# State-space stage with 16 heads: its scores as 64-row products of two heads, its mixing as 32-column products of four heads

## Chip, core and metric

The kernel runs on one core of one Trainium2 chip. The time is that of one execution on the device in microseconds (us). Engines are named as in the profile: PE is the array for matrix products (PEld its weight loads), DVE the vector engine, ACT the engine for activation functions, POOL the general one, SP the queue that issues transfers.

## The reference, cut to what matters

A network of four layers runs over 16 sequences of 256 rows of 128 channels. The change touches one block of it, a state-space block with 16 heads, a state of 64 and an inner width of 256, so 16 channels a head. For head h and time steps t and s of one sequence:

    decay[h, s, t]  = exp(cum[h, t] - cum[h, s])   for s <= t, else 0     (cum: running sum of log decays)
    score[h, s, t]  = sum over 64 states of b[h, state, s] * c[h, state, t]
    y[h, d, t]      = sum over s of x[h, s, d] * decay[h, s, t] * score[h, s, t]        d = 0 .. 15
    out             = rms_norm(y * sigmoid(gate)) @ w_out

b, c, x, gate and the step sizes are projections of the normalised input; x also goes through a short causal convolution and silu. Nothing of this changes.

## The kernel before

The program is a row of stages; the edited one is made by `ssm_block(..., heads=16, mamba=False)`, whose tiles carry the prefix `ssm_`. A second stage, with 4 heads (`mamba=True`, prefix `mamba_`), comes from the same function. The stage works through eight pairs of sequences (PAIRS = 8). A pair has 512 rows: two sequences j = 0, 1 of 256, each two tiles of 128.

**Front part of a pair.** PE takes a list of work items in turn through two PSUM banks (`run_item`, lines 1048 to 1107): x (L1062), dt (L1064), sixteen bc items (L1067; eight for c, then eight for b), two gate items (L1069), two turns of x (L1079), and between them, late, turn_y and out (L1090, L1105) of the pair before. ACT and DVE empty the banks. A b item holds the 64 states of two heads below each other and goes to `b_rows` in one operation. A c item holds two heads in the same way, but L1263 writes it in two operations of 64 rows: the lower head to `c_rows[0:64, 0]`, the upper one to `c_rows[64:128, 1]`. The other halves of `c_rows` stay zero (memset at L1326). DVE meanwhile runs the convolution and the chain of running sums (L1388 to L1420), which ends in `parts`.

**Units.** A unit is one head of one sequence; 32 a pair (u = 16 j + h), 256 in all.

- The fade: six bf16 products (L1128, L1130, L1132, once for 256 and once for 128 columns) put cum[t] - cum[s] for the three blocks on and above the diagonal, 384 columns, into one of two banks `dbank[u % 2]`. ACT takes the exponential into `decay[u % 2]` (L1281).
- The scores: L1150 (256 columns) and L1151 (128 columns) into `gbank[u % 2]`. All 128 rows of `b_rows` are stationary, with two heads in them; the zeros of `c_rows` cancel the other head.
- The mixer: DVE multiplies decay and score, 128 x 384 (L1465), into `mixer[u % 2]`, then drains and signals `scores_taken`.
- The mixing: L1164 and L1165 add x times mixer for this head into `ybank`. Stationary is a 128-column tile of `x_wide` with the head's 16 channels in place and zeros in the other 112 columns. So the eight heads of a half (EACH = 8, CH = 2) accumulate into the same 128 rows of PSUM.

PE runs one unit ahead: `unit(u + 1)`, then `mix(u)` (L1185 to L1193). Float32 products show as two passes each in the profile (x2 in a row of the timeline), bf16 ones as one.

**Other work between the units.** After unit 15, DVE gates the first sequence (`take_gated`, L1353); ACT squares it after the decay of unit 17, and PE sums the squares (turn_y) ahead of the mixing of unit 19. In pairs 1 to 7, DVE does the tail of the pair before between mixers (L1472 to L1479): after u = 1 the scaling and the first norm's moments, after u = 4 the norm, the addition to x and the next moments, after u = 7 the next norm (`tail_at`, L927). PE turns that result after u = 10 and ACT stores it.

Four waits bound how far the engines run apart: ACT's decay of unit u waits for mixer u - 2, PE's fade of u for decay u - 2, PE's scores of u for mixer u - 2 (`scores_taken`), DVE's mixer of u for mixing u - 2 (`y_up`).

Of the kernel before, what the change touches and what calls it, by code (L numbers as in the profile page):

```python
# [15 lines left out]
ALU = mybir.AluOpType  # L16
ACT = mybir.ActivationFunctionType
# [883 lines left out]
def ssm_block(core, name, tail, heads, mamba):  # L901
# [26 lines left out]
    with ExitStack() as ctx:  # L928
# [13 lines left out]
        else:  # L942

            x_wide = sb("x_wide", [P, PT, CH, EACH * (P + HD)])

            b_rows, c_rows = sb("b_rows", [P, bc_items // 2, PN]), sb("c_rows", [P, 2, bc_items // 2, PN])
# [7 lines left out]
        decay, mixer = sb("decay", [P, 2, SPAN]), sb("mixer", [P, 2, SPAN])  # L954
# [87 lines left out]
        def _(pe):  # L1042
# [71 lines left out]
            def pair(i, has_late):  # L1114
# [3 lines left out]
                def unit(u):  # L1118

                    j, h = divmod(u, heads)  # L1120
                    n = i * units + u
# [3 lines left out]
                    if not (isinstance(i, int) and u < 2):  # L1125
                        pe.wait_ge(decay_done, n - 1)
# [7 lines left out]
                    if mamba and h:  # L1134
                        return
                    if mamba:
                        b, c = bc[0:STATE, 0, :], bc[0:STATE, 1, :]
                        turn_no = i * 2 + j
                        skip = isinstance(i, int) and j < 1
                        need = turn_no  # L1140
                        gb = gbank[0]
                    else:
                        b, c = b_rows[:, h // 2, :], c_rows[:, h % 2, h // 2, :]
                        skip = isinstance(i, int) and u < 2
                        need = n - 1
                        gb = gbank[u % 2]

                    if not skip:
                        pe.wait_ge(scores_taken, need)
                    pe.matmul(gb[:, 0:SEQ], b[:, s[0]:s[0] + P], c[:, s[0]:s[0] + SEQ], start=True, stop=True)  # L1150
                    pe.matmul(gb[:, SEQ:SPAN], b[:, s[1]:s[1] + P], c[:, s[1]:s[1] + P], start=True,  # L1151
                              stop=True).then_inc(scores_up, 1)

                def mix(u):
# [6 lines left out]
                    if not mamba:  # L1161
                        c, k = divmod(h, EACH)
                        x = [x_wide[:, 2 * j + t, c, k * P:(k + 1) * P] for t in range(2)]
                        pe.matmul(ybank[:, c * SEQ:(c + 1) * SEQ], x[0], m[:, 0:SEQ], start=(k == 0), stop=False)  # L1164
# [21 lines left out]
                for u in range(units):  # L1186
                    if u + 1 < units:
                        unit(u + 1)
# [2274 lines left out]
```

## Time and profile before

| | |
|---|---|
| median of 3 runs | 5105.25 us (5102.89 to 5107.88) |
| profiled execution, its own time | 5086.59 us |
| its span | 5084.6 us |
| busy: PE, PEld, DVE, ACT, POOL | 77%, 53%, 51%, 44%, 21% of the span |
| granted TensorE clock, mean | 0.863 of full speed |

The sum of the prediction is made against the profiled execution and carried over to the median. The stage lies from about 2676 to 3535 us. A busy PE is a modelled figure: the end of a matmul's row lies some tenths of a us after its columns are through, so starts of rows are compared, not ends. An engine's idle time stands in brackets, with what ended it.

### The profile page before, as it was taken

To read this page: it belongs to the slowest core of one execution; us is meant where nothing else is said; L and a number is where in the kernel's file an instruction comes from. 1 tells how busy PE (TensorE), PEld (TensorE's weight loads), DVE (VectorE), ACT (ScalarE), POOL (GpSimd) and SP (SyncE) were. 2 spreads that over 40 slices of the span, in tenths; PEclk is the share of its full clock that TensorE was granted. 3 is DMA by queue.
4 is the path that set the end of the run, shared out by engine and by line. 5 is a ranking of instruction groups with operands and counts; after the bars stand their busy time and mean duration, and the time that the engine had idled before them with its cause. 6 is when DMAs were issued, how large, how long until landed. Compare 5 with 4: busy or idle time off the path is not lost. (4 is left out here: it accounts for less than half of the span.)

```text
span 5084.6 us, 65295 instructions
## 1 busy us (share of the span) xinstructions
PE 3893.2 (77%) x19738; PEld 2713.3 (53%) x19800; DVE 2569.9 (51%) x6625; ACT 2231.9 (44%) x4312; POOL 1045.3 (21%) x1066
## 2 busy tenths in 40 slices
PE   3659954999967688878877888987999877720398
PEld 1137722677734455546555667765677555520266
DVE  5858744222234766477864343342222255579544
ACT  3446533333442688778863433342333333300133
POOL 1012211000001666366640000000000000154200
PEclk9879977899976799989998999998999966655599
DMA  1420021000000000000000000000000000000000
GB/s 38 76 51 7 6 75 54 1 0 0 0 20 0 18 1 0 1 18 1 0 1 16 1 0 0 0 0 33 1 0 0 5 1 0 0 1 0 18 0 17
DMA packets 45622, 58.55 MB, mean 12 GB/s; under 512 B 14058, under 2 KB 37836, under 8 KB 44588
## 3 DMA queue, kind: packets, MB, share of 16 engines
q1 hardware_dynamic: 38956, 50.63, 3.6%
q10 hardware_dynamic: 6528, 6.29, 0.8%
q8 instruction: 61, 1.00, 0.1%
q14 instruction: 77, 0.63, 0.0%
HBM read 34.87 MB, written 10.51 MB: 9 GB/s over the span
## 5 line engine op out<-in xcount | busy, mean ns | idle before, releaser
L418 PEld LDWEIGHTS bank<-moe_w,moe_hidden 128*128 128x128 f32 x5376 | 626.6, 192 | 78.6 <-issue 76.4
L418 PE MATMUL bank<-moe_w,moe_hidden 128*128 128x128 f32 x5376 | 630.3, 275 | 0.0
L408 PE MATMUL bank<-normed_t,moe_w 128*128 (+1 forms) x1344 | 613.9, 599 | 11.0 <-ACT moe_hidden L470 7.6
L470 ACT ACTIVATE moe_hidden<-bank,moe_b 128x512 f32<-128x512 f32 x544 | 372.8, 687 | 504.0 <-PE bank L408 502.5
L546 DVE SCALAR_TENSOR_TENSOR branch<-bank,moe_weights,branch 128x128 f32<-128x128 f32 x768 | 216.2, 344 | 708.1 <-PE bank L418 704.1
L90 POOL TENSOR_TENSOR branch_norm_shifted<-branch_norm_moments,eps 128x4 f32<-128x4 f32 x64 | 12.8, 200 | 1914.0 <-DVE branch_norm_moments L83 1914.0
L408 PEld LDWEIGHTS bank<-normed_t,moe_w 128*128 128x128 f32 x1344 | 244.3, 192 | 254.6 <-issue 239.3
L1960 POOL TENSOR_TENSOR local_size<-local_size,local_half_powers 128x8 f32<-128x8 f32 x128 | 257.2, 2009 | 199.7 <-DVE local_size L2026 195.7
L1465 DVE TENSOR_TENSOR ssm_mixer<-ssm_decay,bank 128x384 f32<-128x384 f32 x256 | 141.8, 554 | 300.8 <-PE bank L1151 263.2
L1281 ACT ACTIVATE ssm_decay<-bank 128x384 f32<-128x384 f32 x256 | 124.9, 491 | 327.4 <-PE bank L1132 327.3
L1664 PE MATMUL bank<-local_wqkv,local_shifted 128*128 128x512 f32 x384 | 211.8, 644 | 58.7 <-ACTq L1837 23.9
L843 PE MATMUL bank<-ident,attn_scaled 128*128 128x128 f32 x32 | 8.9, 432 | 250.0 <-DVE attn_scaled L808 250.0
L1848 ACT ACTIVATE local_probs<-bank,local_peak 128x128 f32<-128x128 f32 x512 | 182.1, 379 | 8.5 <-issue 8.4
L1067 PE MATMUL bank<-ssm_in_rows,ssm_wbc 128*128 128x512 f32 x256 | 142.7, 676 | 45.1 <-ACTq L1264 45.1
L1164 PE MATMUL bank<-ssm_mixer,ssm_x_wide 128*128 128x256 f32 x512 | 158.8, 392 | 19.5 <-DVE ssm_mixer L1465 19.5
L1150 PE MATMUL bank<-ssm_c_rows,ssm_b_rows 128*128 128x256 f32 x512 | 173.2, 421 | 0.0
L1952 POOL TENSOR_TENSOR local_turned_part<-local_raw,local_tables 128x512 f32<-128x512 f32 x128 | 165.8, 1295 | 28.0 <-ACT local_raw L1827 26.8
L1689 PE MATMUL bank<-local_k_t,local_q_t 128*128 128x128 f32 x1024 | 139.8, 281 | 23.7 <-ACT local_probs L1848 20.8
L1689 PEld LDWEIGHTS bank<-local_k_t,local_q_t 128*128 128x128 f32 x1024 | 139.4, 198 | 28.0 <-issue 20.8
L1965 POOL TENSOR_TENSOR local_probs<-local_probs,local_total 128x512 f32<-128x512 f32 x128 | 133.2, 1041 | 81.6 <-DVE local_total L2050 81.6
L2045 DVE TENSOR_REDUCE local_peak<-bank 128x4 f32<-128x512 f32 x128 | 88.5, 691 | 114.6 <-PE bank L1689 107.3
L470 ACT ACTIVATE moe_hidden<-bank 128x512 f32<-128x512 f32 x128 | 76.5, 597 | 152.1 <-PE bank L408 152.1
(535 smaller groups left out, 8933.4 us busy)
## 6 DMA issues: line engine op xcount, KB each, us to landing
rwkv_kept<-rwkv_keep SPq DMA_DIRECT2D x8, 768.0 KB, 15.2
moe_w<-in_moe_w_dram SPq DMA_DIRECT2D x2, 2304.0 KB
rwkv_gate<-rwkv_kept SPq DMA_DIRECT2D x8, 512.0 KB, 3.6
moe_w<-in_moe_w_dram SPq DMA_DIRECT2D x2, 2048.0 KB
rwkv_values<-rwkv_sent_v ACTq DMA_DIRECT2D x16, 128.0 KB
normed_t<-rwkv_sent_b SPq DMA_DIRECT2D x16, 128.0 KB
x<-rwkv_sent_w ACTq DMA_DIRECT2D x16, 128.0 KB
rwkv_recv<-rwkv_sent_r SPq DMA_DIRECT2D x16, 128.0 KB
```

What stands on the lines that cost most here:

```text
L408: pe.matmul(hbank[n % 4][:], w1[:, e, f * P:(f + 1) * P], source_t[:, bass.ds(i * PN, PN)], start=True, stop=True).then_inc(hidden_up, 1)
L418: last = pe.matmul(obank[e % 2][:, t * P:(t + 1) * P], hid[:, e % 2, f, t * P:(t + 1) * P], w2[:, e, f, :], start=(f == 0), stop=(f == chu ...
L470: act.activation(hid[:, e % 2, f, :], hbank[n % 4][:], ACT.Gelu_apprx_tanh, bias=b1[:, n:n + 1] if bias else 0.0).then_inc(hidden_done, 1)
L546: last = dve.scalar_tensor_tensor(core.branch[:, t, :], obank[e % 2][:, t * P:(t + 1) * P], weights[:, i * PT + t, e - first_routed:e - fi ...
L1067: last = pe.matmul(bank[0:rows, :], wbc[:, n, :], source, start=True, stop=True)
L1150: pe.matmul(gb[:, 0:SEQ], b[:, s[0]:s[0] + P], c[:, s[0]:s[0] + SEQ], start=True, stop=True)
L1164: pe.matmul(ybank[:, c * SEQ:(c + 1) * SEQ], x[0], m[:, 0:SEQ], start=(k == 0), stop=False)
L1664: pe.matmul(bank[:], shifted[:, at, t * P:(t + 1) * P], wqkv[:, part * INNER:(part + 1) * INNER], start=True, stop=True).then_inc(a_up, 1)
L1689: last = pe.matmul(bank[:, w * P:(w + 1) * P], q_t[:, j, c, w, :], keys, start=False, stop=(w == WINDOWS - 1))
L1848: last = act.activation(probs[:, u % 2, w, :], sbank[u % 2][:, w * P:(w + 1) * P], ACT.Exp, bias=peak[:, u % 2, w:w + 1], accum_out=total[ ...
L1952: pool.tensor_tensor(turned_part[:, m % 2, :].rearrange("p (h s d) -> p h s d", s=2, d=HD // 2), rows, sines.broadcast_to([P, HEADS, 2, HD ...
L1960: pool.tensor_tensor(part, part, half_powers[:], ALU.pow).then_inc(scaled, 1)
```

## The change

- `c_rows` loses its zero halves: [128, 8, 512] in place of [128, 2, 8, 512]. A c item is stored by one ACT operation of 128 rows, as a b item is. The memset on DVE goes.
- Scores of two heads h and h + 1 are issued together (`two_units`): their fades first, then products on rows 0 to 63 (into bank 0) and on rows 64 to 127 (into bank 1), long parts first. PE now waits on `mixer_done` for the bank; DVE's drain and its separate signal go.
- `x_wide` holds 32 columns a head: its own 16 and 16 zeros. `mixer` has 16 slots in place of 2. The mixing of eight heads is issued at once (`mix_octet`): 16 products with 32 stationary columns, four of them to rows 0, 32, 64 and 96 of `ybank` in turn. The two heads of a group of 32 rows accumulate. DVE waits for an octet's mixing, two octets back, once per eight units; PE mixes octet o after the block of units 8 (o + 1) + 2 and + 3 has been issued, the last one at the end of the pair.
- x is copied to `x_wide` by two half-size copies per item in place of one. Gating the first sequence moves from after unit 15 to after unit 20; squaring from 17 to 21, turn_y from 19 to 22, its store from 20 to 24; ACT's store of the turned tail from u = 10 to u = 12.

```diff
-            x_wide = sb("x_wide", [P, PT, CH, EACH * (P + HD)])
-            b_rows, c_rows = sb("b_rows", [P, bc_items // 2, PN]), sb("c_rows", [P, 2, bc_items // 2, PN])
+            x_wide = sb("x_wide", [P, PT, CH, EACH, 2 * HD])
+            b_rows, c_rows = sb("b_rows", [P, bc_items // 2, PN]), sb("c_rows", [P, bc_items // 2, PN])
...
-        decay, mixer = sb("decay", [P, 2, SPAN]), sb("mixer", [P, 2, SPAN])
+        decay, mixer = sb("decay", [P, 2, SPAN]), sb("mixer", [P, 2 if mamba else 2 * EACH, SPAN])
...
+                def two_units(u):
+                    fade(u)
+                    fade(u + 1)
+                    j, h = divmod(u, heads)
+                    s = [j * SEQ, j * SEQ + P]
+                    for part, (to, rows, width) in enumerate(((0, s[0], SEQ), (SEQ, s[1], P))):
+                        for k in range(2):
+                            if part == 0 and not (isinstance(i, int) and u < 2):
+                                pe.wait_ge(mixer_done, i * units + u + k - 1)
+                            low = slice(k * STATE, (k + 1) * STATE)
+                            last = pe.matmul(gbank[k][:, to:to + width], b_rows[low, h // 2, rows:rows + P],
+                                             c_rows[low, h // 2, rows:rows + width], start=True, stop=True)
+                            if part:
+                                last.then_inc(scores_up, 1)
+
+                def mix_octet(o):
+                    j, c = divmod(o, CH)
+                    pe.wait_ge(mixer_done, i * units + (o + 1) * EACH)
+                    if c == 0 and not (isinstance(i, int) and j == 0):
+                        pe.wait_ge(y_taken, i * 2 + j)
+                    for b in range(2):
+                        for part, (to, at) in enumerate(((slice(0, SEQ), slice(0, SEQ)),
+                                                         (slice(P, SEQ), slice(SEQ, SPAN)))):
+                            for g in range(EACH // 2):
+                                h = 2 * g + b
+                                last = pe.matmul(ybank[g * 2 * HD:(g + 1) * 2 * HD, c * SEQ + to.start:c * SEQ + to.stop],
+                                                 x_wide[:, 2 * j + part, c, h, :], mixer[:, (o % 2) * EACH + h, at],
+                                                 start=(b == 0 and part == 0), stop=(b == 1 and part == 1))
+                    last.then_inc(y_up, 1)
...
+                two_units(0)
+                for u in range(0, units, 2):
+                    if u + 2 < units:
+                        two_units(u + 2)
+                    if u % EACH == 0 and u:
+                        mix_octet(u // EACH - 1)
+                    if u == heads + 6:
                         item("turn_y", 0)
-                    mix(u)
-                    if u == tail_at[3] and has_late and tail.turned:
+                    if u == tail_at[3] and has_late:
                         tail.pe(pe, i - 1)
+                mix_octet(units // EACH - 1)
...
-                        for half in range(2):
-                            low = slice(half * STATE, (half + 1) * STATE)
-                            act.activation(c_rows[low, half, b - bc_items // 2, :], bank[low, :], ACT.Identity)
-                        act.drain()
-                        act.sem_inc(sign, 1)
+                        act.activation(c_rows[:, b - bc_items // 2, :], bank[:], ACT.Identity).then_inc(sign, 1)
...
-            if not mamba:
-                dve.memset(c_rows[:], 0.0)
...
-                        out = x_wide[:, :, c].rearrange("p t (h k) -> p t h k", k=P + HD)[:, :, :, 0:HD]
-                        ins = dve.tensor_copy(out, bank.rearrange("p t (h d) -> p t h d", d=HD))
+                        own = x_wide[:, :, c].rearrange("p t (g b) k -> p t g (b k)", b=2)
+                        new = bank.rearrange("p t (g b d) -> p t g b d", b=2, d=HD)
+                        for b in range(2):
+                            at = b * 3 * HD
+                            ins = dve.tensor_copy(own[:, :, :, at:at + HD], new[:, :, :, b, :])
...
-                    if u >= 2:
+                    if mamba and u >= 2:
                         dve.wait_ge(y_up, n - 1)
-                    ins = dve.tensor_tensor(mixer[:, u % 2, :], decay[:, u % 2, :], scored, ALU.mult)
-                    ins.then_inc(mixer_done, 1)
-                    if not mamba:
-                        dve.drain()
-                        dve.sem_inc(scores_taken, 1)
-                    if u == heads - 1:
+                    if not mamba and u % EACH == 0 and u >= 2 * EACH:
+                        dve.wait_ge(y_up, i * 2 * CH + u // EACH - 1)
+                    slot = u % 2 if mamba else u % (2 * EACH)
+                    dve.tensor_tensor(mixer[:, slot, :], decay[:, u % 2, :], scored, ALU.mult).then_inc(mixer_done, 1)
+                    if u == (heads - 1 if mamba else heads + 4):
                         take_gated(i, 0)
```

## Rows read from the trace of the kernel before

**Rows 1.** The page, part 1: busy us, share of the span, instructions of each engine.

```profile
PE 3893.2 (77%) x19738; PEld 2713.3 (53%) x19800; DVE 2569.9 (51%) x6625; ACT 2231.9 (44%) x4312; POOL 1045.3 (21%) x1066
```

**Rows 2.** Windows: units of pairs 0 and 1, busy time, clock, DMA.

```profile
core 0: us, PE busy (x) PEld busy (x) DVE busy (x) ACT busy (x) POOL busy (x), PEclk, DMA share, GB/s
2724.60:2787.10 62.50, 62.05 (x456) 56.47 (x456) 18.84 (x34) 16.40 (x34) 0.00 (x0) 0.96 0.00 1
...
2825.60:2891.00 65.40, 62.34 (x460) 56.34 (x460) 25.07 (x63) 18.07 (x36) 2.42 (x4) 0.98 0.00 1
```

**Rows 3.** Timeline of one steady unit: start us, us, engine, line, operation.

```profile
2737.35 0.28 PE L1128 MATMUL bank<-ssm_parts,ssm_pick 96*128 96x256 bf16 x1
...
2737.75 0.22 PE L1132 MATMUL bank<-ssm_future,ssm_ident 128*128 128x128 bf16 x1
2737.81 0.65 PE L1150 MATMUL bank<-ssm_c_rows,ssm_b_rows 128*128 128x256 f32 x2
2738.29 0.38 PE L1151 MATMUL bank<-ssm_c_rows,ssm_b_rows 128*128 128x128 f32 x2
2738.51 0.60 PE L1164 MATMUL bank<-ssm_mixer,ssm_x_wide 128*128 128x256 f32 x2
2738.71 0.55 DVE L1465 TENSOR_TENSOR ssm_mixer<-ssm_decay,bank 128x384 f32<-128x384 f32 x1 [1.26 <-PE bank L1151]
2738.95 0.38 PE L1165 MATMUL bank<-ssm_mixer,ssm_x_wide 128*128 128x128 f32 x2
2739.17 0.28 PE L1128 MATMUL bank<-ssm_parts,ssm_pick 96*128 96x256 bf16 x1
2739.28 0.27 PE L1130 MATMUL bank<-ssm_unpick,ssm_parts 96*128 96x256 bf16 x1
```

**Rows 4.** Timeline of pair 1's first units, DVE first, then PE.

```profile
2829.63 0.55 DVE L1465 TENSOR_TENSOR ssm_mixer<-ssm_decay,bank 128x384 f32<-128x384 f32 x1 [0.49 <-PE bank L1151]
...
2832.94 0.55 DVE L1465 TENSOR_TENSOR ssm_mixer<-ssm_decay,bank 128x384 f32<-128x384 f32 x1 [0.26 <-issue]
...
2835.67 0.55 DVE L1465 TENSOR_TENSOR ssm_mixer<-ssm_decay,bank 128x384 f32<-128x384 f32 x1 [1.31 <-PE bank L1151]
...
2840.21 0.55 DVE L1465 TENSOR_TENSOR ssm_mixer<-ssm_decay,bank 128x384 f32<-128x384 f32 x1 [0.26 <-issue]
...
2843.69 1.11 DVE L99 TENSOR_SCALAR fresh<-x,x_norm_moments,x_norm_rstd 128x128 f32 x4 [0.21 <-issue]
...
2840.81 0.70 PE L1164 MATMUL bank<-ssm_mixer,ssm_x_wide 128*128 128x256 f32 x2 [1.56 <-DVE ssm_mixer L1465]
...
2848.82 0.27 PE L1128 MATMUL bank<-ssm_parts,ssm_pick 96*128 96x256 bf16 x1
```

**Rows 5.** Timeline of PE in the stage with 4 heads, a change of tile shape.

```profile
4229.56 0.22 PE L1132 MATMUL bank<-mamba_future,mamba_ident 128*128 128x128 bf16 x1
...
4230.24 0.38 PE L1151 MATMUL bank<-mamba_bc 64*128 64x128 f32 x2
...
4230.67 0.27 PE L1130 MATMUL bank<-mamba_unpick,mamba_parts 96*128 96x256 bf16 x1
```

**Rows 6.** Timeline of PE, one idle stretch; then windows, as rows 2, at half clock.

```profile
2796.26 2.08 PE L1067 MATMUL bank<-ssm_in_rows,ssm_wbc 128*128 128x512 f32 x2 [4.23 <-ACTq L1264]
...
2794.70:2804.90 10.20, 8.38 (x28) 6.61 (x29) 7.12 (x14) 4.37 (x9) 2.02 (x3) 0.50 0.00 1
4078.00:4112.00 34.00, 28.29 (x120) 21.70 (x120) 11.03 (x34) 5.81 (x11) 1.56 (x4) 0.50 0.00 1
```

**Rows 7.** Timeline of pair 1's front: a c item on ACT, bc items on PE.

```profile
2808.07 1.20 ACT L1263 ACTIVATE ssm_c_rows<-bank 64x512 f32<-64x512 f32 x2 [0.16 <-issue]
...
2812.06 6.85 PE L1067 MATMUL bank<-ssm_in_rows,ssm_wbc 128*128 128x512 f32 x14 [0.23 <-ACTq L1264]
```

**Rows 8.** Timeline: copies to x_wide, the stage's memset; DMA issues, us to landing.

```profile
2824.14 1.29 DVE L1447 COPY ssm_x_wide<-bank 128x512 f32<-128x512 f32 x2 [4.50 <-PE bank L1079]
...
2678.33 7.77 POOL L1018 MEMSET ssm_x_wide<- 128x9216 f32 x1
...
ssm_future<-in_future_dram SPq DMA_DIRECT2D x1, 32.0 KB, 4.0
```

More of the change, by code:

```diff
@@ L1116, in item, with fade @@
                     run_item(i, kind, n)
-                def unit(u):
+                def fade(u):
                     j, h = divmod(u, heads)
-                    n = i * units + u
                     s = [j * SEQ, j * SEQ + P]
@@ L1133, in unit @@
                     last.then_inc(decay_up, 1)
-                    if mamba and h:
+                def unit(u):
+                    fade(u)
+                    j = u // heads
+                    if u % heads:
                         return
[L1136 to L1151, printed above, removed]
-                              stop=True).then_inc(scores_up, 1)
+                    if not (isinstance(i, int) and u < heads):
+                        pe.wait_ge(scores_taken, i * 2 + j)
+                    b, c, s = bc[0:STATE, 0, :], bc[0:STATE, 1, :], [j * SEQ, j * SEQ + P]
@@ L1184, in pair @@
                     pe.wait_ge(down[side], before + 1)
-                unit(0)
-                for u in range(units):
-                    if u + 1 < units:
-                        unit(u + 1)
-                    if u == heads + (0 if mamba else 3):
+                if mamba:
+                    unit(0)
+                    for u in range(units):
+                        if u + 1 < units:
+                            unit(u + 1)
+                        if u == heads:
+                            item("turn_y", 0)
+                        mix(u)
+                        if u == tail_at[3] and has_late and tail.turned:
+                            tail.pe(pe, i - 1)
+                    return
+                two_units(0)
[5 more added lines that the diff above has]
+                    if u == heads + 6:
                         item("turn_y", 0)
-                    mix(u)
-                    if u == tail_at[3] and has_late and tail.turned:
+                    if u == tail_at[3] and has_late:
                         tail.pe(pe, i - 1)
+                mix_octet(units // EACH - 1)
             pair(0, False)
@@ L1281, in pair @@
                     act.activation(decay[:, u % 2, :], dbank[u % 2][:, 0:SPAN], ACT.Exp).then_inc(decay_done, 1)
-                    if u == heads + 1 and not mamba:
+                    if u == heads + 5 and not mamba:
                         square(i, 0)
-                    if u == heads + (1 if mamba else 4):
+                    if u == heads + (1 if mamba else 8):
                         turned_y(i, 0)
-                    if u == tail_at[3] and has_late and tail.turned:
+                    if u == tail_at[3] + (0 if mamba else 2) and has_late and tail.turned:
                         tail.act(act, i - 1)
@@ L1344, in take_gated @@
             def take_gated(i, j):
-                dve.wait_ge(y_up, i * units + (j + 1) * heads)
+                dve.wait_ge(y_up, i * units + (j + 1) * heads if mamba else i * 2 * CH + (j + 1) * CH)
                 if mamba:
```

14 lines of the change are left out of this document (5 added, 9 removed).

## The prediction

> **What bounds the kernel now.** I read, in this order: the page's busy times, the windows of single stretches, the timeline of one unit, the lines around the same operations in the other state-space stage, and the timelines of DVE and ACT. Over the whole span no engine but PE is near full [rows 1], but that is an average over eight stages; only one of them is edited. In it each of the eight pairs has a front part (projections, convolution) and 32 units. In the units of pair 0 PE is busy 62.05 of 62.50 us, DVE 18.84, ACT 16.40; in pair 1, 62.34 of 65.40, DVE 25.07, ACT 18.07 [rows 2]. So the array bounds the units. One steady unit lasts 1.82 us from L1128 to L1128: 0.46 for the six bf16 products of the fade (2737.35 to 2737.81), 0.70 for the scores (to 2738.51), 0.66 for the mixing (to 2739.17) [rows 3]. Every float32 product is two passes; from L1164 to L1165 is 0.44, so a pass of 256 columns costs 0.22, one of 128 costs 0.11. Nothing waits in this chain: time goes with streamed columns, whether rows of the array carry zeros (scores) or columns do (mixing). In pairs 1 to 7 the remaining 3 us come from DVE's tail work: the mixing at 2840.81 waited 1.56 us for the mixer [rows 4].
>
> **The fade** is untouched: 0.46 a unit.
>
> **Scores.** A block of two units now issues four products, tile 0, tile 1, then the short ones. Serially their passes are 4 x 0.22 + 4 x 0.11 = 1.32, what two units cost now (less the 0.05 that the first load sticks out). The trace has no two products in flight on different rows, so I bound it. Above: 1.32, no overlap. Below: if tiles ran with no regard to order, half, 0.66. Between: PE starts passes in program order [rows 3], and the second pass of a product needs the tile of its first; then only second pass and next product's first overlap. That gives starts 0, 0.22, 0.22, 0.43, 0.43, 0.54, 0.65, 0.76 and an end at 0.87; if each 128-column load (one pass of 128 columns long, estimate 0.11, since L1165's passes with their loads follow every 0.11) starts only with the previous pass, 1.08. I take 0.97.
>
> **Mixing.** An octet is 16 products of 32 stationary columns. Serially 8 x (0.44 + 0.22) = 5.28, as now. With neighbours overlapping as above, 8 x (0.22 + 0.11) = 2.64, plus up to 0.03 a product for the short loads: 3.1. I take 2.85. Four at a time without regard to order would be 1.32.
>
> The Trainium skill ("TensorE: Matmul & The Clock Gate", Part 3) reports matmuls on distinct row or column groups starting some 4 ns apart, with 2.38x for three column tiles and 3.07x for four row tiles; by its span model alone scores and mixing would take the lower ends. No run here shows this yet, and it does not speak of products made of two passes.
>
> **Change of tile shape.** The stage with 4 heads already has 64-row scores between full-height products. From L1132 to L1151 there is 4229.56 to 4230.24, 0.68; without a change of shape 2737.75 to 2738.29, 0.54. Going in costs 0.14. From L1151 to L1130 is 4230.24 to 4230.67, 0.43; from L1165 to L1130 2738.95 to 2739.28, 0.33. Going out costs 0.10 [rows 3, 5]. The Trainium skill ("TensorEngine Tiling (Array Packing)", Key Properties) says that changing the mode drains TensorE: a rule against this change, and the trace agrees, at 0.1 us a time. A block then costs 2 x 0.46 + 0.14 + 0.97 + 0.10 = 2.13 against 2 x 1.16 now; an octet's mixing 2.85 + 0.17 = 3.02 against 5.28.
>
> **Does DVE or ACT become the bound?** A mixer takes 0.55 and starts 0.20 after its scores' passes end (L1151's end 2738.51, DVE starts 2738.71); PE resumes 0.05 after a mixer (2840.76 to 2840.81) [rows 3, 4]. The second mixer of a block ends 0.2 + 0.55 + 0.4 = 1.15 after the scores; PE comes back to that bank after 0.10 + 0.92 + 0.14 + 0.22 = 1.38. No stall in steady state, with 0.2 to spare. The removed drain and separate semaphore make DVE only faster. With DVE's tail work it is otherwise. After mixer 1 there is a block of work to 2832.94 (2.8 us), after mixer 4 one of 4.0 us (2836.22 to 2840.21), after mixer 7 four scalings, 1.4 with their waits [rows 4]. The first octet so holds 8 x 0.57 + 8.2 = 12.8 us of DVE work with two score banks between it and PE. Walking it: scores 2 and 3 wait for nothing, 4 and 5 end at 9.5, mixer 4 ends at 10.1, the long block at 14.1, mixer 5 at 14.7, scores 6 and 7 at 15.4, mixer 9 at 19.05, scores 10 and 11 at 19.75, and octet 0 is mixed at 22.9. Now: unit 11 begins at 2848.82, 23.2 after 2825.6; with its 1.16 and less the two mixings ahead, 23.1 for the same work. **Octet 0 of pairs 1 to 7 gains nothing.** PE idles there some 3.6 us at a stretch. After 4.23 us of such idling the granted clock was 0.50, the 1.2 GHz level, for 10.2 us [rows 6]; here it may be 0 to 3.4 us dearer, and I take 1.7.
>
> **The rest of a pair**: ten blocks 21.3, three mixings 9.1, side jobs (turns, gating) 2.6, and 1.2 at the end, where the last mixing waits for both last mixers and nothing covers it: 34.2 against 65.4 - 23.1 = 42.3. Gain 8.1 - 1.7 + 0.2 = 6.6 a pair, 46 over seven (I take the later pairs as pair 1). Pair 0: 16 x 2.13 + 4 x 3.02 + 2.5 (start at half clock) + 1.6 + 1.2 = 51.5 against 62.5, gain 11.
>
> **Front.** A c item took two half-height ACT operations, 1.20 + 0.16 = 1.36 per item, and PE waited for it; b items pass at 6.85 / 7 = 0.98 [rows 7]. With one operation of 0.60 PE bounds c items too: five items x 0.4, and 0.6 on the first ones, 2.7 us a pair (2 in pair 0): 21. DVE is through with its chain by then, so nothing is behind it. The x_wide copies, 1.29 for two, become four half as long; each instruction adds some 0.05, and PE waits for them: -0.1 a pair, -0.8 [rows 8]. At the start POOL's memset (7.77, to 2686.10) shrinks to 2/9 and DVE's goes, but the last load lands 4.0 after its issue, about 0.3 us earlier than POOL is done: 0.3, ends 0 and 0.4. Queues: SP's loads are the same, POOL's work otherwise too.
>
> Sum: 46 + 11 + 21 - 0.8 + 0.3 = 77. The profiled execution took 5086.6 (span 5084.6), so it becomes 5009.5; the median of the three runs is 18.7 above it, and I forecast **5028** for the median. Its own range: low terms (0.87, 2.64, no loss of clock) 28 less, 5000; high ones 5057.
>
> **Rivals.**
> Tiles do not overlap at all. Then shape changes are pure loss: blocks 2.48, mixings 5.45, 13.3 a pair worse than forecast in pairs 1 to 7, 15 in pair 0, net +31: 5136, slower. For it: the trace shows every pass waiting for the one before. Against: bf16 passes start every 0.06 us, so issue is no limit. It decides once less than 0.3 of the overlap assumed (worth 108 us in all) is there. Chance 0.09.
> Only rows overlap: 32 x 2.43 lost, 5106, no change: 0.06. Only columns: 86 blocks x 0.35, 5058: 0.08.
> Overlap by the tile count (0.66 and 1.35): then DVE's loop of 1.85 bounds the block: 86 x 0.28 + 32 x 1.5 = 72 more, 4956: 0.06. The span model of the Trainium skill ("TensorE: Matmul & The Clock Gate", Part 3) leads here.
> The clock stays at half through the units. In the stage with 4 heads it was 0.50 over 34 us in which PE was busy 28.29 [rows 6]. Blocks would cost 3.95, mixings 2.6 more: +161, 5266. Against: here streamed passes fill most of the time, and it was 0.98 in units that held the 1.56 us wait [rows 2, 4]. Chance 0.03.
> The forecast has 0.68.
>
> **Numbers.** A measurement of this kernel tells about 0.2%, 10 us. Faster: 0.68 + 0.08 + 0.06 = 0.82; same 0.06; slower 0.12. The range 4980 to 5112 holds forecast, only-columns and only-rows (0.82) with the unknown ends; the no-overlap and half-clock cases and the full overlap are left out.
>
> **What would show it.** In the new profile: score products with 64 rows whose starts lie 0.22 apart for three passes of which two start together (overlap) or each 0.22 apart (none); blocks near 2.13; 32-column products every 0.22 to 0.25 in long form; octets 3.0; in octet 0 an idle PE of 3 to 4 us before a score product, released by DVE; the c items at 0.96; units of pair 1 near 59, of pair 0 near 51.5. I am wrong if units of pair 0 stay above 58, or if the granted clock of the units falls below 0.9.

## The result, and the profile after

The changed kernel took **4937.97 us** in the median of 4 runs (4936.23 to 4945.66), the kernel before 5104.07 beside it on the same chip (5098.09 to 5107.88): ratio 0.968, 95% interval 0.966 to 0.970. Run again later it took 4945.10 against 5097.57, ratio 0.970 (0.969 to 0.972). It is faster, as forecast, but by 166 us where 77 were forecast, and the time lies below the range.

The profiled execution took 4945.66 (span 4943.9). The unedited stages together took 4237.9 before and 4250.5 after, and between 4237 and 4271 in the profiled executions of the runs below, so I compare the edited stage by itself, from its first to its last instruction: 846.7 us before, 693.4 after, **-153.3**. By where each pair's first fade and last mixing stand, this splits as follows (a stretch of units runs from the first to the end of the second):

| | before | after | |
|---|---|---|---|
| units of pair 0 | 62.5 | 42.4 | -20.1 |
| units of pairs 1 to 7, each | 65.3 to 66.0 | 50.8 | -103.9 in all |
| the seven stretches between them | 268.7 | 243.1 | -25.6 |
| up to the first unit | 48.0 | 44.3 | -3.7 |

What follows the last unit took 8.1 before and 8.2 after.

The page after, part 1, answers to [rows 1]: PE is 146 us less busy, at the same number of instructions.

```profile
PE 3746.8 (76%) x19738; PEld 2542.2 (51%) x19800; DVE 2553.2 (52%) x6640; ACT 2187.2 (44%) x4248; POOL 1043.4 (21%) x1066
```

The windows after: units of pair 0, units of pair 1, and 6.8 us inside the latter (columns as in [rows 2]).

```profile
2733.60:2775.90 42.30, 40.81 (x457) 32.26 (x457) 17.42 (x34) 15.71 (x34) 0.00 (x0) 0.93 0.01 2
2811.80:2862.50 50.70, 45.42 (x461) 34.99 (x461) 23.70 (x63) 17.49 (x36) 2.41 (x4) 0.87 0.00 1
2824.50:2831.30 6.80, 6.07 (x34) 4.64 (x35) 3.60 (x9) 1.49 (x4) 1.17 (x2) 0.51 0.01 2
```

PE still bounds most of the units. The timeline of PE after, three blocks of two units and one octet's mixing in pair 0, answers to [rows 3].

```profile
2741.90 0.28 PE L1127 MATMUL bank<-ssm_parts,ssm_pick 96*128 96x256 bf16 x1
...
2742.91 0.92 PE L1158 MATMUL bank<-ssm_c_rows,ssm_b_rows 64*128 64x256 f32 x8
2743.76 0.28 PE L1127 MATMUL bank<-ssm_parts,ssm_pick 96*128 96x256 bf16 x1
...
2744.76 1.09 PE L1158 MATMUL bank<-ssm_c_rows,ssm_b_rows 64*128 64x256 f32 x8
2745.78 0.28 PE L1127 MATMUL bank<-ssm_parts,ssm_pick 96*128 96x256 bf16 x1
...
2746.78 0.92 PE L1158 MATMUL bank<-ssm_c_rows,ssm_b_rows 64*128 64x256 f32 x8
2747.64 1.51 PE L1174 MATMUL bank<-ssm_mixer,ssm_x_wide 128*32 128x256 f32 x32
2749.08 0.28 PE L1127 MATMUL bank<-ssm_parts,ssm_pick 96*128 96x256 bf16 x1
```

The first block lasts 1.86 from L1127 to L1127: 1.01 up to the first score pass, 0.85 from there to the next fade. The second lasts 2.02, with 1.02 from its first score pass to the next fade. In the steady stretches blocks of the two lengths take turns. A mixing of eight heads lasts 1.44 from its first pass to the next fade. It lengthens the third block from 1.86 to 3.30, so an octet costs 1.44.

What makes every second block 0.16 longer is a wait for DVE that no bracket shows, because passes of the other tile keep PE busy. The timeline of DVE after, the mixers of the first two blocks, two in each row:

```profile
2743.86 1.02 DVE L1496 TENSOR_TENSOR ssm_mixer<-ssm_decay,bank 128x384 f32<-128x384 f32 x2 [1.01 <-PE bank L1158]
2745.72 1.02 DVE L1496 TENSOR_TENSOR ssm_mixer<-ssm_decay,bank 128x384 f32<-128x384 f32 x2 [0.84 <-PE bank L1158]
```

In the second block the first head's first pass starts at 2744.763 and the second head's at .934, 55 ns after the second mixer of the block before (2744.879) has freed its bank. Five or six of a pair's sixteen blocks are held in this way, which adds up to 5.7 us over the stage.

The single passes in the trace say how the rest comes about. The eight score passes of the first block start in four couples, one on each tile, 7 ns apart: 2742.905 and .912, 2743.225 and .232, .441 and .448, .550 and .557. The 32 mixing passes start in eight groups of four, 6 to 7 ns apart, every 0.22 (256 columns; 0.24 after the very first) or 0.11 (128): 2747.638, .645, .651 and .658 are the first passes of four different products, and their second passes follow together from .878.

The lines by form after, over the stage: mean ns of one pass stands before the second bar.

```profile
L1496 DVE TENSOR_TENSOR ssm_mixer<-ssm_decay,bank 128x384 f32<-128x384 f32 x256 | 133.2, 552 | 202.8 <-PE bank L1158 179.5 <-ACT ssm_decay L1308 17.8 <-issue 5.5
L1158 PE MATMUL bank<-ssm_c_rows,ssm_b_rows 64*128 64x256 f32 x512 | 123.5, 482 | 23.8 <-DVE ssm_mixer L1496 23.8
L1174 PE MATMUL bank<-ssm_mixer,ssm_x_wide 128*32 128x256 f32 x512 | 40.1, 385 | 7.5 <-DVE ssm_mixer L1496 7.5
L1292 ACT ACTIVATE ssm_c_rows<-bank 128x512 f32<-128x512 f32 x64 | 37.3, 596 | 28.7 <-PE bank L1067 26.9 <-issue 1.8
```

PE's new waits, as far as brackets show them, are the 23.8 before score products and the 7.5 before mixings. The timeline of PE after, the end of pair 0 and the worst wait of pair 1's first octet:

```profile
2774.43 1.51 PE L1174 MATMUL bank<-ssm_mixer,ssm_x_wide 128*32 128x256 f32 x32 [0.94 <-DVE ssm_mixer L1496]
...
2825.23 1.64 PE L1158 MATMUL bank<-ssm_c_rows,ssm_b_rows 64*128 64x256 f32 x6 [2.90 <-DVE ssm_mixer L1496]
```

The timeline of DVE after, in the same octet, answers to [rows 4]: between the mixers that start at 2820.52 and 2824.62 stands the long piece of tail work.

```profile
2818.70 1.02 DVE L1496 TENSOR_TENSOR ssm_mixer<-ssm_decay,bank 128x384 f32<-128x384 f32 x2 [0.24 <-issue]
2820.52 0.56 DVE L1496 TENSOR_TENSOR ssm_mixer<-ssm_decay,bank 128x384 f32<-128x384 f32 x1 [0.80 <-PE bank L1158]
...
2824.62 0.56 DVE L1496 TENSOR_TENSOR ssm_mixer<-ssm_decay,bank 128x384 f32<-128x384 f32 x1 [0.23 <-issue]
2826.50 1.02 DVE L1496 TENSOR_TENSOR ssm_mixer<-ssm_decay,bank 128x384 f32<-128x384 f32 x2 [1.33 <-PE bank L1158]
```

In the front part, c items pass every 0.86 to 1.00 (ACT after, against [rows 7]), and there ACT waits for PE. One wait of PE for ACT stays in each pair, ahead of the third c item: 3.60, where it was 4.23 [rows 6].

```profile
2794.81 0.60 ACT L1292 ACTIVATE ssm_c_rows<-bank 128x512 f32<-128x512 f32 x1 [0.40 <-PE bank L1067]
2795.67 0.60 ACT L1292 ACTIVATE ssm_c_rows<-bank 128x512 f32<-128x512 f32 x1 [0.26 <-PE bank L1067]
2796.62 0.60 ACT L1292 ACTIVATE ssm_c_rows<-bank 128x512 f32<-128x512 f32 x1 [0.36 <-PE bank L1067]
```

### The profile page after: what moved, and what is told of

It is laid out like the page before. It is cut to its first block and busy times, and to the rows that moved or that the text cites. A ratio compares the mean times of both kernels' runs of the same rounds, so it can differ in the third digit from the quotient of the medians.

```text
span 4943.9 us, 64940 instructions
## 1 busy us (share of the span) xinstructions
PE 3746.8 (76%) x19738; PEld 2542.2 (51%) x19800; DVE 2553.2 (52%) x6640; ACT 2187.2 (44%) x4248; POOL 1043.4 (21%) x1066
## 5 line engine op out<-in xcount | busy, mean ns | idle before, releaser
L1158 PE MATMUL bank<-ssm_c_rows,ssm_b_rows 64*128 64x256 f32 (+1 forms) x1024 | 156.3, 391 | 23.8 <-DVE ssm_mixer L1496 23.8
L1067 PE MATMUL bank<-ssm_in_rows,ssm_wbc 128*128 128x512 f32 x256 | 131.7, 660 | 30.0 <-ACT ssm_c_rows L1292 30.0
L1127 PE MATMUL bank<-ssm_parts,ssm_pick 96*128 96x256 bf16 (+1 forms) x512 | 136.1, 273 | 15.6 <-DVE ssm_x_wide L1475 8.6
```

The lines of the kernel that those rows point to most:

```text
L1127: pe.matmul(bank[:, col:col + width], pick[:, h, :], parts[:, rows:rows + width], start=True, stop=False)
L1158: last = pe.matmul(gbank[k][:, to:to + width], b_rows[low, h // 2, rows:rows + P], c_rows[low, h // 2, rows:rows + width], start=True, sto ...
```

## Experiments

Each is the changed kernel with one edit. Two questions lead: by what rule does the array start products on different tiles (the step that failed), and what is each other part worth? "Stage" is always the edited stage by itself, 693.4 us in the changed kernel.

### Scores head by head

```diff
-                    for part, (to, rows, width) in enumerate(((0, s[0], SEQ), (SEQ, s[1], P))):
-                        for k in range(2):
+                    for k in range(2):
+                        for part, (to, rows, width) in enumerate(((0, s[0], SEQ), (SEQ, s[1], P))):
```

> The changed kernel with the four score products of a block in another order: both of head k (rows 0 to 63), then both of head k + 1 (rows 64 to 127). Theory A, tiles drain on their own: each tile takes its passes as they come and products of the other tile are not held by them; a block stays at 1.86 us and the time within 10 us of the changed kernel (4938). Theory B, passes start in program order and one that needs a busy tile holds all behind it: six of eight passes run alone, a block costs about 2.4 us, 96 + blocks lose 0.5 each, and the kernel takes 4975 to 4995 us.

Measured: 4942.25 us, ratio 0.970 (0.967 to 0.973), stage 692.7, blocks of 1.86 and 2.01 in turn. The order is now long and short of head k, then long and short of head k + 1, and still the long ones start together: 2743.549 and .562 (in a block that follows an octet's mixing, where DVE holds nothing up). The second head's product started 13 ns after the first one's, while the first head's short product was still waiting for its tile. So a product whose tile is free passes one that waits.

### Mixing group by group

```diff
-                    for b in range(2):
-                        for part, (to, at) in enumerate(...):
-                            for g in range(EACH // 2):
+                    for g in range(EACH // 2):
+                        for b in range(2):
+                            for part, (to, at) in enumerate(...):
```

> The changed kernel with the 16 mixing products of an octet in another order: all four of a group of 32 columns, then the next group. Theory A (tiles drain on their own): mixing stays at about 1.4 us an octet, time as the changed kernel, 4938. Theory B (program order, a busy tile holds all behind it): within a group nothing overlaps, an octet costs about 5.0 us, 3.6 more, 32 times, 115 us: 5050.

Measured: 5007.41 us, ratio 0.982 (0.978 to 0.985), stage 756.1. Neither theory's number: an octet costs 3.46. The timeline of PE of this kernel, a block and an octet:

```profile
2746.00 0.93 PE L1158 MATMUL bank<-ssm_c_rows,ssm_b_rows 64*128 64x256 f32 x8
2746.86 3.53 PE L1174 MATMUL bank<-ssm_mixer,ssm_x_wide 128*32 128x256 f32 x32
2750.32 0.28 PE L1127 MATMUL bank<-ssm_parts,ssm_pick 96*128 96x256 bf16 x1
```

Of group 0, four products for one tile, the first long one starts at 2746.858, its short one at 2747.314, the second long one at .533 and its short one at .964. Group 1's first starts at .538: with group 0's third, past its fourth, but not before. The trace does not name the group of a pass, but only one short product has started when the third long one does, so a later product has overtaken group 0's second short one. It could pass one waiting product, not two. That gave a new theory, which the next run tests.

### Mixing with two products of a tile in a row

```diff
-                        for part, (to, at) in enumerate(...):
-                            for g in range(EACH // 2):
+                        for g in range(EACH // 2):
+                            for part, (to, at) in enumerate(...):
```

> The changed kernel with the mixing products ordered head pair by head pair: for each group of 32 columns the long and the short product, then the next group. Theory C, read from the two orders run before: a product may start past one waiting product of another tile, not past two. Then the third product (group 1, long) starts with the first, the fifth only with the second, and an octet takes 1.9 to 2.2 us against 1.44 (all four groups in turn) and 3.6 (group by group): 15 to 25 us above the changed kernel, 4953 to 4963. Theory A, tiles drain on their own without such a bound: 1.44, 4938. Theory B, program order: 0.44 + 0.22 per pair less one overlap, some 4 us an octet, 5020.

Measured: 4945.86 us, ratio 0.969 (0.965 to 0.972), stage 693.8, an octet 1.48. The timeline of PE of this kernel, a block and an octet:

```profile
2742.49 0.92 PE L1158 MATMUL bank<-ssm_c_rows,ssm_b_rows 64*128 64x256 f32 x8
2743.34 1.54 PE L1174 MATMUL bank<-ssm_mixer,ssm_x_wide 128*32 128x256 f32 x32
2744.82 0.28 PE L1127 MATMUL bank<-ssm_parts,ssm_pick 96*128 96x256 bf16 x1
```

The four groups start at 2743.344, .357, .370 and .384, the last one past three waiting products of other tiles. The theory of the last run, with its 1.9 to 2.2, is refuted, and so is a limit on waiting products over all tiles. What is left is a limit on how many there are for one tile, and the next run tests it.

### Mixing with three products of a tile in a row

```diff
-                    for b in range(2):
-                        for part, (to, at) in enumerate(...):
-                            for g in range(EACH // 2):
...
+                    three = [(g, b, part) for g in range(EACH // 2) for b, part in ((0, 0), (0, 1), (1, 0))]
+                    for g, b, part in three + [(g, 1, 1) for g in range(EACH // 2)]:
```

> The changed kernel with the mixing products ordered so that each group of 32 columns gets its first three in a row, then the last ones of all four groups follow. Theory D, formed after group by group (3.6 us an octet) and two by two (1.5): each tile holds one product at work and one waiting; a third for the same tile stops the queue for all tiles until the first is through. Then the first long products of the groups start 0.43 us apart (with the second product of the group before them), an octet takes about 2.7 us, 1.2 more than in the changed kernel, some 35 us in all: 4975. Theory A (no such bound): 1.44 and 4938. A bound on waiting products over all tiles together, at two: two by two would have shown it.

Measured: 5009.03 us, ratio 0.984 (0.982 to 0.985), stage 741.2. The timeline of PE of this kernel:

```profile
2743.14 1.09 PE L1158 MATMUL bank<-ssm_c_rows,ssm_b_rows 64*128 64x256 f32 x8
2744.16 2.87 PE L1174 MATMUL bank<-ssm_mixer,ssm_x_wide 128*32 128x256 f32 x32
2746.97 0.28 PE L1127 MATMUL bank<-ssm_parts,ssm_pick 96*128 96x256 bf16 x1
```

The groups' first products start at 2744.160, .621, 2745.083 and .545, 0.46 apart: each when the group before has brought its second product to work (2744.615), so that its third takes the waiting place. An octet costs 2.81 where about 2.7 was expected, and the pattern is the one that the rule gives: **a tile holds one product at work and one that waits; a third for the same tile holds up everything behind it.** Every product here is two passes, so these runs do not tell a limit of two products from one of four passes.

The stage got 48 us longer, 44 of them from the octets (32 x 1.37). The median is 71 above the changed kernel's and missed the expected 4975. The profiled execution, at 4979.56, was the fastest of five and the others took 5007.67 to 5014.42; where those spent the other 30 us is open.

### Scores on all 128 rows, as before

```diff
-                            last = pe.matmul(gbank[k][:, to:to + width], b_rows[low, h // 2, rows:rows + P],
-                                             c_rows[low, h // 2, rows:rows + width], start=True, stop=True)
+                            last = pe.matmul(gbank[k][:, to:to + width], b_rows[:, h // 2, rows:rows + P],
+                                             c_rows[:, k, h // 2, rows:rows + width], start=True, stop=True)
```

c_rows has its zero halves and ACT's two stores again.

> The changed kernel with the scores and c_rows of the kernel before (128 rows with zeros, c in two operations and a memset), order and mixing as changed. If the overlap of the two row tiles is what the scores' part brings: a block 0.9 + 1.35 = 2.25 to 2.3 us in place of 1.86, some 80 of 128 blocks not hidden behind DVE, 33 us, and 25 to 30 us in the front parts: 4995 to 5005. If row tiles bring little because of two changes of shape a block, the blocks stay below 2.0 and only the front's 25 to 30 us come back: 4965.

Measured: 5012.07 us, ratio 0.983 (0.980 to 0.987), stage 757.8: units of pair 0 47.9, of later pairs 54.2 to 55.8, stretches between them 270.6 in all. The timeline of PE of this kernel, one block:

```profile
2740.61 1.52 PE L1158 MATMUL bank<-ssm_c_rows,ssm_b_rows 128*128 128x256 f32 x8
2741.97 0.27 PE L1127 MATMUL bank<-ssm_parts,ssm_pick 96*128 96x256 bf16 x1
```

From the first score pass to the next fade it is 1.36 where the tiled scores have 0.85 or, held by DVE, 1.02; the whole block is 2.26 (0.90 + 1.36). So the tiled scores save 0.40 or 0.24 a block of two, and 35 us of units in all; the other 27.5 are the front part.

### Mixing on all 128 columns, as before

```diff
-                                last = pe.matmul(ybank[g * 2 * HD:(g + 1) * 2 * HD, c * SEQ + to.start:c * SEQ + to.stop],
-                                                 x_wide[:, 2 * j + part, c, h, :], mixer[:, (o % 2) * EACH + h, at],
+                                last = pe.matmul(ybank[:, c * SEQ + to.start:c * SEQ + to.stop],
+                                                 x_wide[:, 2 * j + part, c, h * P:(h + 1) * P], mixer[:, (o % 2) * EACH + h, at],
...
```

x_wide has its layout of before; the order by octets stays.

> The changed kernel with the mixing products of the kernel before (128 stationary columns with zeros), still eight heads at once. If four column tiles really run together: an octet's mixing goes from 1.44 to 5.3 us, 3.8 x 32 = 122 us: 5060. If the gain of the mixing came from issuing it by octets (fewer waits) and not from the tiles: within 30 us of the changed kernel.

Measured: 5074.18 us, ratio 0.995 (0.993 to 0.997), stage 823.4, units 57.9 and 66.0 to 66.6. The timeline of PE of this kernel, one octet:

```profile
2746.30 5.50 PE L1174 MATMUL bank<-ssm_mixer,ssm_x_wide 128*128 128x256 f32 x32
2751.64 0.27 PE L1127 MATMUL bank<-ssm_parts,ssm_pick 96*128 96x256 bf16 x1
```

From its first pass to the next fade an octet takes 5.34 (2746.30 to 2751.64) in place of 1.44: 125 us of units. The mixing is the larger part by far.

### Both on the full array: the order alone

This run leaves out the zeros: the scores use all 128 rows of both operands, so each score is the sum over two heads. The front part stays the changed kernel's, and only the order by blocks and octets is left of the change to the units.

```diff
-                            last = pe.matmul(gbank[k][:, to:to + width], b_rows[low, h // 2, rows:rows + P],
-                                             c_rows[low, h // 2, rows:rows + width], start=True, stop=True)
+                            last = pe.matmul(gbank[k][:, to:to + width], b_rows[:, h // 2, rows:rows + P],
+                                             c_rows[:, h // 2, rows:rows + width], start=True, stop=True)
```

and the edit of the run before.

> The changed kernel with scores on all 128 rows (without zeros, so each score is the sum over two heads; this part of the computation is changed) and mixing on all 128 columns; only the order by blocks and octets is left of the change to the units. The two parts undone one at a time lengthened a unit part of pair 0 by 5.5 and 15.5 us and of pairs 1 to 7 by 4 and 15.4. Theory E (the order by octets costs something where DVE's tail work stands between the mixers, since only half of the mixings are left to cover it): units of pair 0 about 63.4, of later pairs about 70, against 62.5 and 65.4 before; fronts stay 34.5 to 35.8; the stage about 153 above the changed kernel less some 7, near 845, and the median about 5085. Rival (the order costs nothing, the two parts only overlap in what they save): later pairs 65.5 to 66.5, the stage near 815, the median about 5055.

Measured: 5094.54 us, ratio 1.000 (0.999 to 1.002), stage 838.1. The windows of this kernel, units of pairs 0 and 1:

```profile
2729.50:2792.50 63.00, 61.53 (x457) 55.82 (x458) 17.43 (x35) 15.63 (x34) 0.00 (x0) 0.96 0.00 1
2828.10:2896.20 68.10, 62.62 (x461) 56.26 (x462) 23.65 (x64) 17.40 (x36) 2.41 (x4) 0.96 0.00 1
```

Pair 0 costs 63.0 against 62.5 before, later pairs 68.1 to 69.7 against 65.3 to 66.0. In pair 1 PE is busy as long as before (62.62 against 62.34), but the units last 2.7 us longer: one wait of 3.13 for a mixer stands in the first octet, where the longest before was 1.56. That fits the theory that the mixings which used to cover DVE's tail work now come at the end of an octet. So the order has a price, 21 us of units, about two thirds of what the theory gave and more than the rival's. The saved front time, 28 us, pays for it. From here to the changed kernel the tiles are worth 145 us of units, 21 more than the 124 that the units gained in all.

### A c item in two operations

```diff
-                        act.activation(c_rows[:, b - bc_items // 2, :], bank[:], ACT.Identity).then_inc(sign, 1)
+                        for half in range(2):
+                            low = slice(half * STATE, (half + 1) * STATE)
+                            act.activation(c_rows[low, b - bc_items // 2, :], bank[low, :], ACT.Identity)
+                        act.drain()
+                        act.sem_inc(sign, 1)
```

> The changed kernel with each c item stored by two ACT operations of 64 rows and a drain, as before, into the new c_rows. Only the front parts can change. If one operation for two explains the front's gain (34.5 us against 38.0 to 38.9 between the units of two pairs), fronts go back to about 38 and the kernel loses 20 to 28 us: 4960 to 4966. If the fronts got shorter because the first products of the next pair no longer wait for DVE's copy at the end of the units, it loses under 8 us.

Measured: 4971.25 us, ratio 0.975 (0.972 to 0.978), stage 717.2, the stretches between units 265.3 in all against 243.1, the units nearly unchanged (396.9 against 397.9). The timeline of ACT of this kernel shows items every 1.36 again:

```profile
2792.08 1.20 ACT L1294 ACTIVATE ssm_c_rows<-bank 64x512 f32<-64x512 f32 x2 [0.16 <-issue]
2793.43 1.20 ACT L1294 ACTIVATE ssm_c_rows<-bank 64x512 f32<-64x512 f32 x2 [0.16 <-issue]
```

One operation in place of two is worth 23.8 us of the stage. In the front part alone it is 24.7 (22.2 between units, 2.5 ahead of the first), most of the 29.3 gained there (25.6 + 3.7); where the other 4.6 come from was not tested.

### DVE's tail work later, and earlier

```diff
-    tail_at = (0, 2, 4, 6) if mamba else (1, 4, 7, 10)
+    tail_at = (0, 2, 4, 6) if mamba else (11, 19, 27, 28)
```

> The changed kernel with the tail work of the pair before moved on DVE from after units 1, 4 and 7 to after units 11, 19 and 27, each just where PE has an octet to mix, and PE's turn from after 10 to after 28. Nothing is left out. Theory: units of pairs 1 to 7 take 50.8 us against 42.4 in pair 0 because DVE's tail work holds the mixers while PE has only two score banks, and because the granted clock falls to half after PE's wait of 2.9 us. Then units of pair 1 come to 44 to 46 us, no half clock inside them but at the start, and the kernel gains 35 to 45 us: 4895 to 4905. Rival: the work costs DVE the same wherever it stands, and the loss only moves: within 10 us of 4938.

Measured: 4942.67 us, ratio 0.970 (0.967 to 0.973), stage 676.1. The expected 4895 to 4905 was missed. Pair 1 did as expected, with units of 45.7, and so did pairs 3, 5 and 7 (45.5), but pairs 2, 4 and 6 took 49.8. A window of this kernel in the units of pair 2:

```profile
2904.00:2922.00 18.00, 16.56 (x153) 12.34 (x152) 8.94 (x26) 4.46 (x10) 1.21 (x2) 0.72 0.00 0
```

The granted clock was 0.50 from 2910.3 to 2920.5, the lower level, 1.2 GHz. PE was busy for 16.56 of the 18 us, but just before the fall it had been idle for 1.44 of 2.1 us, in two waits for mixers (0.70 up to 2909.03 and 0.74 up to 2910.46) with two score passes between them. The run shows the fall, not its cause. A last variant keeps the tail work early, but spreads it:

```diff
-    tail_at = (0, 2, 4, 6) if mamba else (1, 4, 7, 10)
+    tail_at = (0, 2, 4, 6) if mamba else (3, 11, 15, 18)
```

> The changed kernel with the tail work on DVE after units 3, 11 and 15 and PE's turn after 18. Nothing is left out. The spread over 11, 19 and 27 took 45.7 us for the units of pair 1 but 49.8 in pairs 2 to 7, where the clock fell beside the 1-column products of turn_y. Theory (DVE's 2.8, 4.0 and 1.4 us hold PE, and the clock falls where two such waits meet): kept clear of gating and turn_y, units of all later pairs take 46 to 47.5 us without half clock inside, and the stage gets 25 to 32 us shorter: 4906 to 4913. Rival (any place costs the same in the end): units 49.5 to 51 and 4938.

Measured: 4929.30 us, ratio 0.968 (0.966 to 0.970), stage 667.2, all later pairs 46.1 to 46.2. So its stage is 26 us shorter, as expected, but the time is above the expected 4906 to 4913, and one set of runs could not tell the whole kernel from the changed one. Both were run again on one chip.

> The changed kernel, unchanged, beside the next one on the same chip. Expected 4938 to 4944 in the median, stage 693.

> The changed kernel with DVE's tail work after units 3, 11, 15 and 18 in place of 1, 4, 7 and 10. One run showed the stage 26 us shorter, the whole kernel 12 to 15 shorter with times that scattered. If the stage's gain reaches the end: 26 below after_again, about 4914 against 4940. Rival (the other stages give it back, their spans being 10 to 15 longer): the two medians within 10 of each other.

Measured: 4945.10 us, ratio 0.970 (0.969 to 0.972), and 4929.26 us, ratio 0.967 (0.965 to 0.968): the intervals do not meet, and the spread tail is 16 us (0.3%) faster, between the 26 of the theory and the rival's 10. Its stage was 667.3 again. The window of the second kernel over pair 1's units, against 50.70 us at clock 0.87 in the changed one:

```profile
2819.70:2865.90 46.20, 42.48 (x461) 33.36 (x461) 23.52 (x63) 17.41 (x36) 2.42 (x4) 0.93 0.01 2
```

The units give 32 us less in all, the stretches between them take back 8; why a third of the stage's gain does not reach the end of the kernel is within what the other stages wander and stays open.

## Why the prediction was wrong in size and right in sign

**What bounds the units** held: 62 of 62.5 us busy meant that streamed passes were the time, and taking them off the path took the time off. With both on the full array PE was again busy for 61.53 of 63.00 us in pair 0.

**Scores, the failed step.** "PE starts passes in program order [rows 3], and the second pass of a product needs the tile of its first; then only second pass and next product's first overlap." I took 0.97 for four products. Measured from the starts: 0.32 + 0.216 + 0.109 + 0.109 = 0.754. Each couple is together on its two tiles. What is left above the lower end of 0.66 is 0.10 on the first pass; the weight load for the second pass ends at 2743.198 and that pass starts at .225, so the load is the likely cause, which no run tests. The block is 1.86, or 2.02 where DVE holds the second head, instead of 2.13.

**Mixing, the same step, and most of the error.** I took 2.85, with 0.17 for the shape (a term without a working) 3.02; measured 1.44, of which the passes are 1.34 and going out 0.10. The lower end of 1.35 was the true value, and I had put it into a rival at 0.06. Between ends of 5.28 and 1.32 I chose by a rule of order read from [rows 3], where all products use the whole array: those rows could not tell order from need of the same tile. The experiments with the changed orders show which it is.

The Trainium skill ("TensorE: Matmul & The Clock Gate", Part 3) reports distinct tiles starting some 4 ns apart, and 2.38x for three column tiles. The runs here agree with the first in kind, at 7 ns, and give more than the second: the passes of an octet went from 5.24 in the run with both on the full array to 1.34, 3.9x for four column tiles. The same part says that matmuls start strictly in the order of the program. The run with the mixing group by group speaks against it: group 1's first product started at 2747.538, group 0's fourth at 2747.964.

**The shape change** was priced nearly rightly. From the first pass of a mixing to the next fade there is 0.10 more than its passes need, and a block with tiled scores is 1.01 + 0.85 against 0.92 + 0.754 for its parts, so 0.19 for both ways; the 0.24 taken also held 0.05 of the first load. Going from the scores to a mixing costs no more than going from them to a fade (0.85 either way), so an octet adds one change, 0.10, where 0.17 was taken. In these runs, then, every change shows as a gap of some 0.1.

**Does DVE become the bound?** "No stall in steady state, with 0.2 to spare" was wrong. PE was to come back to the second head's bank after 0.10 + 0.92 + 0.14 + 0.22 = 1.38. The 0.22 held the second head one pass behind the first, by the same rule of order, and without it PE is back after 1.10. The second mixer ends 1.21 after the scores, and PE resumes 0.055 later: some 0.17 of stall in every second block. So the rival was right that DVE's loop would bind once the tiles overlap; the loop is 2.02 where it had 1.85, and it binds every other time.

**Octet 0 of pairs 1 to 7 gains nothing** was nearly right. Unit 12 starts 22.3 us after unit 0, where I had 22.9, and 24.6 with the clock's 1.7; the same work took 23.1 before. PE idled 2.90 before the product at 2825.23 (forecast some 3.6). In the half-clock window that begins during this wait, the next two intervals are 3.40 and 3.88 where pair 0 has 2.02 and 3.30: 2.0 us lost, 1.7 forecast. The two runs with the tail work moved confirm the cause, since they free 4.6 to 5.1 us in pair 1 (50.8 to 46.2 and 45.7).

**The rest of a pair** came to 28.5 instead of 34.2, 5.7 less. The terms alone say 7.4: 10 blocks x 0.27 + 3 mixings x 1.58. The 1.7 between them are 0.7 for second heads held by DVE, and the rest where PE now meets DVE's and ACT's side work. With octet 0's 2.3 the 5.7 are the 8.0 by which the pair (50.8 against 58.8) was missed. Over seven pairs this is 56 of the error; pair 0, 42.4 against 51.5, is 9 more.

**Front.** Forecast 21 + 0.3 - 0.8; measured 25.6 + 3.7. The run with two operations shows the cause of most of it, 24.7. The four half-size copies of x_wide start 0.33 to 0.34 apart and take 1.42 in all against 1.29 for the two of before: 0.13 a pair, where 0.1 was forecast.

**In all**: 56 + 9 + 9 = 74 of the 76 us of stage time that the forecast missed (77 against 153). The rival "overlap by the tile count", at 4956, is what happened; of the 18 us below it the front is 9; the rest lies within what the other stages wander. Against the forecasts of what would show: blocks near 2.13 (1.86 and 2.02), octets 3.0 (1.44), the idle stretch in octet 0 (2.90), c items at 0.96 (0.86 to 1.00), units at 59 and 51.5 (50.8 and 42.4).

The range was too narrow for a reason that the text itself had: the low terms gave 28 us, as they held 2.64 for an octet whose lower end had been written down as 1.32. With that end, and no loss of clock, it would have reached 5028 - 72 - 12 = 4944, and the rival's own sum was 4956.

## What to carry to other kernels

Where small products leave rows or columns of the array idle, put them on tiles, and issue them so that no tile gets a third product while others are idle: in turn or two in a row, never a whole group at once. When a cost is bounded from rows that cannot tell two rules apart, give the far end a real chance and let the range reach it. And when the bounding engine gets faster, the side work of the next one (here DVE's tail work in the first octet) becomes the wait; spread it over units that have room.

## What the runs showed of the hardware that was not expected

- A product on a free tile starts past waiting products of other tiles, up to three in these runs. Each tile takes one product at work and one waiting (a product is two passes here); an octet costs 1.44 with products in turn, 1.48 with two in a row, 2.81 with three, 3.46 with four.
- The passes of float32 products on different tiles interleave: the first passes of four products start 7 ns apart (13 ns with two in a row), then their second passes do.
- Four column tiles gave 3.9x on the passes, two row tiles 1.8x (1.36 for serial scores, 0.754 for tiled ones).
- A wait can hide behind the other tile: in every second steady block the second head's product started 0.17 late, and PE's row has no bracket.
- Beginning in a wait of 2.90 us the granted clock stood at half for 6.8 us. With the tail work late it stood at half for 10.2 us in every second pair, after two waits of 0.70 and 0.74 close together. With both on the full array, a wait of 3.13 was followed by 3.4 us at half (from 3049.1) in pair 3, and the same wait in pair 1 by none. So the length of a wait alone does not decide; what does is open.
